# The first group of a two-layer kernel as eight plain products, with tile 0's parts for the store made later

## The reference, cut to what matters

```python
# x: (B, S, D); B = 2, here S = 1024 tokens, D = 256, F = 1024, E = 8
g = jnp.einsum('bsd,edf->ebsf', h, Wg)
u = jnp.einsum('bsd,edf->ebsf', h, Wu)
expert_outs = jnp.einsum('ebsf,efd->ebsd', jax.nn.silu(g) * u, Wd)
expert_output = jnp.einsum('be,ebsd->bsd', gating_probs, expert_outs)
shared = jnp.einsum('bsf,fd->bsd', jax.nn.silu(h @ Sg) * (h @ Su), Sd)
sg = shared_gate_prob[:, :, None]
return (1.0 - sg) * expert_output + sg * shared      # added to x, then layer 2
...
attn_in = jnp.tanh(jnp.einsum('bsd,da->bsa', hidden, W1) + b1)
scores = jnp.einsum('bsa,a->bs', attn_in, v)
p = jax.nn.softmax(masked_scores, axis=-1)
pooled = jnp.einsum('bjl,bld->bjd', p, hidden) / cnt[..., None]   # added again
```

## Time and profile before

| | |
|---|---|
| time, median of 3 runs | 1097.8 us (1097.63 to 1097.84) |
| the profiled execution | 1097.32 us, of which the span from first to last instruction 1095.6 us |
| busy share of the span | PE 99%, DVE 86%, ACT 68%, POOL 57% |
| matmuls | 4846 |
| DMA | 242.30 MB, 219 GB/s of HBM traffic over the span |

### The profile page before, as it was taken

How to read it: one execution, slowest core, us unless ns; L and a number is a source line. 1 busy time by engine, 2 the same in 40 slices (tenths; PEclk the granted TensorE clock), 3 DMA queues, 4 the chain that set the end, 5 groups by cost and what they waited for, 6 DMA issues and landing times.

```text
span 1095.6 us, 16016 instructions
## 1 busy us (share of the span) xinstructions
PE 1088.1 (99%) x4846; PEld 893.2 (82%) x4846; DVE 946.8 (86%) x1224; ACT 747.6 (68%) x1335; POOL 621.7 (57%) x543
## 2 busy tenths in 40 slices
PE   8999999999999999999999999999999999999998
PEld 6888888888888888888888888888878888888886
DVE  7888888888888888888689999999888999889986
ACT  7777677677777667677666666666656666666666
POOL 7765666656766665656335566555543444454435
PEclk9999999999999999999999999999999999999999
DMA  7776676666676676676675566666545655555522
GB/s 240 236 275 222 241 268 244 241 259 226 240 269 234 252 261 222 243 269 250 259 250 211 212 214 207 207 216 219 201 164 198 212 205 186 209 210 198 196 104 78
DMA packets 82421, 242.30 MB, mean 221 GB/s; under 512 B 23456, under 2 KB 54688, under 8 KB 73120
## 3 DMA queue, kind: packets, MB, share of 16 engines
q1 hardware_dynamic: 81520, 240.75, 61.4%
q10 hardware_dynamic: 816, 0.52, 0.2%
HBM read 134.29 MB, written 105.91 MB: 219 GB/s over the span
## 4 chain that ended last, share of the span: by engine, by line
PE 97%; POOL 1%; DVE 1%; DMA 0%; issue 0%; ACT 0%; ACTq 0%; DVEq 0%; POOLq 0%
PE acc_of L1769 11%; PE acc_of L1771 11%; PE acc_of L1770 11%; PE v_both L1769 9%; PE v_both L1771 9%; PE v_both L1770 9%; PE g_ps L1769 6%; PE e_ps L1769 6%; PE g_ps L1771 6%; PE e_ps L1771 6%; PE g_ps L1770 6%; PE e_ps L1770 6%; DMA raw<-in_L_cond_Wg 0%; POOL raw L645 0%; PE acc_of L2005 0%
## 5 line engine op out<-in xcount | busy, mean ns | idle before, releaser
L1023 ACT ACTIVATE silu<-g_ps 128x512 f32<-128x512 f32 x144 | 86.2, 599 | 171.2 <-PE g_ps L1771 171.0
L1769 PE MATMUL v_both<-xs_hi,wq 128*128 128x512 f32 x432 | 168.6, 390 | 0.1
L1771 PE MATMUL v_both<-xs_lo,wq 128*128 128x512 f32 x432 | 168.1, 389 | 0.0
L1770 PE MATMUL v_both<-xs_hi,wq 128*128 128x512 f32 x432 | 168.1, 389 | 0.0
L1386 DVE TENSOR_TENSOR up<-v_both,p_sb 128x512 f32<-128x512 f32 x144 | 99.2, 689 | 46.2 <-PE v_both L1771 43.1
L848 POOL TENSOR_TENSOR a<-a,a_own 128x512 f32<-128x512 f32 x35 | 56.1, 1604 | 132.4 <-DVE a_own L1413 132.4
L1341 DVE TENSOR_TENSOR wq<-raw,wq 128x896 fp32r<-128x896 f32 (+1 forms) x70 | 123.7, 1768 | 0.0
L1379 DVE TENSOR_TENSOR gate<-e_ps,v_part 128x512 f32<-128x512 f32 x144 | 98.6, 684 | 28.9 <-PE e_ps L1771 27.9
L1029 ACT ACTIVATE p_sb<-e_ps 128x512 f32<-128x512 f32 x144 | 86.3, 599 | 53.4 <-PE e_ps L1771 53.1
L1769 PE MATMUL e_ps<-xs_hi,wq 128*128 128x512 f32 x288 | 112.4, 390 | 0.7 <-POOL wq L640 0.7
L1769 PE MATMUL g_ps<-xs_hi,wq 128*128 128x512 f32 x288 | 112.5, 391 | 0.4 <-ACT v_both L1017 0.4
(11 more groups left out here) (298 smaller groups left out, 2861.2 us busy)
## 6 DMA issues: line engine op xcount, KB each, us to landing
wq_kept<-wq SPq DMA_DIRECT2D x72, 896.0 KB, 4.6
wq<-wq_kept SPq DMA_DIRECT2D x72, 896.0 KB, 4.5
wd_kept<-wd SPq DMA_DIRECT2D x36, 1024.0 KB, 6.5
wd<-wd_kept SPq DMA_DIRECT2D x36, 1024.0 KB, 6.2
raw_d<-in_L_cond_Wd SPq DMA_DIRECT2D x32, 256.0 KB, 4.5
raw<-in_L_cond_Wg SPq DMA_DIRECT2D x31, 256.0 KB, 2.6
raw<-in_L_cond_Wu SPq DMA_DIRECT2D x31, 256.0 KB, 3.3
out_x<-x SPq DMA_DIRECT2D x8, 256.0 KB, 2.1
```

The lines of the kernel that those rows point to most:

```text
L1023: nc.scalar.activation(silu0[:, i % 2, :], g_ps[:], ACT.Silu).then_inc(silu0_done, 1)
L1769: nc.tensor.matmul(ps, w_hi, a_hi, start=start, stop=False, skip_group_check=True)
L1770: nc.tensor.matmul(ps, w_lo, a_hi, start=False, stop=False, skip_group_check=True)
L1771: return nc.tensor.matmul(ps, w_hi, a_lo, start=False, stop=stop, skip_group_check=True)
```

## The change

Group 0 is computed by eight plain products (`first_group`): gate and up of tile 0 for both halves of tokens, with the blocks of Wg, Wu and x as they are. Gate goes to `g_ps` and `e_ps`, up to `v_ps[0]` and to the bank `acc[1][1]`. It needs no sums of x and none of weights. The split blocks of Wu lie in slot 2 of `wq` (`UP0`), a split x block in `h_hi`/`h_lo` (`X21`). p1 of group 1 stands between the third and the fourth pair of products. Then p2, p7 and p6 of group 1 follow, and the loop starts at i = 1. Since group 0 has no p7 and p6 to keep, the counts of several semaphores shift by one.

On GpSimd the split of Wu comes in the place of tile 0's sums, and the sums of both tiles of pair 0 are made by one `combine`. The five other parts of tile 0 are needed in batch 1 only. They are made after the low parts of tile 2, in a place of their own (`w0_parts`, where x lay before its transposition), and SyncE stores them from there. SyncE stores the first two parts at n = 0, waits at n = 1 for the five others, stores them, and then loads pair 2. ScalarE's and VectorE's lists at the start are written in another order, and VectorE's `rest_w` and ScalarE's `round_w` of tile 1 come before the loop.

```diff
+        w0_parts = place("w0_parts", [P, 2, NP - 2, P], F32R, l1_at[1])
...
+        UP0 = [w[:, 0:2, :] for w in weights(2)]
+        UP0_BANK = acc[1][1]
+        X21 = h_hi[1][:, 2, :], h_lo[1][:, 2, :]
...
-        ROUNDED = ((1, 2, 4, 7, 6, 5, 3), (1, 2, 7, 6, 4, 5, 3))
-        COPIED = (1, 4, 2)
+        ROUNDED = ((1, 2, 0, 4, 5, 7, 6, 3), (1, 2, 7, 6, 4, 5, 3))
+        COPIED = (1, 2, 4)
...
-                sp.wait_ge(gu_split, n + 1)
+                if n == 0:
+                    sp.wait_ge(gu0_split, 1)
+                    sp.dma_start(wq_kept[0][:, :, 0:2, :], wq[:, 0, :, 0:2, :].bitcast(F32)).then_inc(wq_stored[0], 16)
+                    continue
+                sp.wait_ge(gu_split, n)
+                if n == 1:
+                    sp.wait_ge(gu0_split, 3)
+                    sp.dma_start(wq_kept[0][:, :, 2:NP, :], w0_parts[:].bitcast(F32)).then_inc(w0_stored, 16)
                 if n % PAIR == PAIR - 1 and m < NU // PAIR:
                     load_gu(sp, m)
...
+                if n == 0:
+                    sp.wait_ge(w0_stored, 16)
...
-                combine(s, slice(0, P))
-                split(w[:, 3:8, :], hi[:, 2:NP, :], lo[:, 2:NP, :], NP - 2, gu_hi_done, 1, gu_split)
+                split(w[:, 0:4:3, :], UP0[0], UP0[1], 2, gu0_hi_done, 2, gu0_split)
                 pool.wait_ge(staged_g[s], 16)
                 pool.wait_ge(staged_u[s], 16)
-                combine(s, slice(P, PAIR * P))
+                combine(s, slice(0, PAIR * P))
...
-                    pool.wait_ge(gu_hi_done, PAIR + 1)
-
-                    pool.wait_ge(gu_split, PAIR)
+                    pool.wait_ge(gu_hi_done, PAIR)
+                    pool.wait_ge(gu_split, PAIR - 1)
                     nc.gpsimd.tensor_tensor(lo[:], raw[:, 1, 1:8, 0:P], hi[:].bitcast(F32), ALU.subtract).then_inc(gu_split, 1)
+                    pool.wait_ge(xT_done, KD * NT)
+                    split(raw[:, 0, 3:8, 0:P], w0_parts[:, 0], w0_parts[:, 1], NP - 2, gu0_hi_done, 3, gu0_split)
...
-                act.wait_ge(t_step, 3 * (n // PAIR + 2 if n >= PAIR else n + 1))
+                act.wait_ge(t_step, 3 * (n // PAIR + 1))
+                if n == 2:
+                    act.wait_ge(p_done[3], 1)
...
+            def gate_second(i):
+                if i == 0:
+                    act.wait_ge(p_done[4], 1)
+                else:
                     act.wait_ge(gate1_done, i)
-                nc.scalar.activation(v_part[:], v_ps[i % 2][:], ACT.Copy).then_inc(v_copied, 1)
-
-            def gate_second(i):
-                act.wait_ge(gate1_done, i + 1)
-                if i:
                     act.wait_ge(h_done[1], i)
-                nc.scalar.activation(silu1[:], gate1[:], ACT.Silu).then_inc(silu1_done, 1)
+                nc.scalar.activation(silu1[:], gate1[:] if i else e_ps[:], ACT.Silu).then_inc(silu1_done, 1)
...
+            act.wait_ge(xT_done, KD + 1)
+            nc.scalar.activation(X21[0], acc[0][1][:], ACT.Copy).then_inc(xs_hi_done[0], 1)
             act.wait_ge(xs_split[0], 1)
             copy_xT(0, BLOCK[1])
-            copy_xT(0, BLOCK[4])
+            round_x(0, 4)
+            act.wait_ge(staged_g[0], 16)
+            nc.scalar.activation(weights(1)[0][:, 0:2, :], raw[:, 0, 1:3, P:PAIR * P], ACT.Copy).then_inc(gu1_hi_done, 1)
             act.wait_ge(xs_split[0], 2)
             copy_xT(0, BLOCK[2])
-            seed(0)
-            round_x(0, 4)
+            gate_first(0)
+            round_x(0, 5)
+            act.wait_ge(xs_split[0], ROUNDED[0].index(4) + 1)
+            copy_xT(0, BLOCK[4])
             round_x(0, 7)
-            act.wait_ge(staged_g[0], 16)
-            nc.scalar.activation(weights(1)[0][:, 0:2, :], raw[:, 0, 1:3, P:PAIR * P], ACT.Copy).then_inc(gu1_hi_done, 1)
-            gate_first(0)
+            round_w(1)
             round_x(0, 6)
-
-            act.wait_ge(s_done[0], SQ[6] + 1)
-            round_x(0, 5)
-            keep_p7(0)
-            round_x(0, 3)
-            keep_v(0)
-            round_w(1)
 
             ROUND_X1 = {X1_AT + 8 + 2 * k: (q,) for k, q in enumerate(ROUNDED[1])}
             for i in range(NU):
                 seed(i + 1)
-                if i == 1:
+                if i == 0:
+                    round_w(2)
+                elif i == 1:
                     round_w(3)
                 gate_second(i)
                 if i == 0:
-                    round_w(2)
+                    round_x(0, 3)
                 elif i == PAIR:
                     round_w(4)
                 gate_first(i + 1)
...
+            dve.wait_ge(xs_hi_done[0], ROUNDED[0].index(0) + 1)
             nc.vector.tensor_copy(half_of(0, 1, 0), acc[0][1][:]).then_inc(xT_own, 1)
-            dve.wait_ge(xT_copied, COPIED.index(4) + 1)
+            nc.vector.tensor_tensor(X21[1], acc[0][1][:], X21[0].bitcast(F32), ALU.subtract).then_inc(xs_split[0], 1)
+            dve.wait_ge(xs_hi_done[0], ROUNDED[0].index(4) + 1)
+            dve.wait_ge(xT_own, 1)
             combine_x(0, 5)
-            dve.wait_ge(xT_own, 1)
+            rest_x(0, 4)
+            dve.wait_ge(gu1_hi_done, 1)
+            nc.vector.tensor_tensor(weights(1)[1][:, 0:2, :], raw[:, 0, 1:3, P:PAIR * P],
+                                    weights(1)[0][:, 0:2, :].bitcast(F32), ALU.subtract).then_inc(gu1_split, 1)
+            dve.wait_ge(xT_copied, COPIED.index(1) + 1)
+            dve.wait_ge(xs_split[0], ROUNDED[0].index(0) + 1)
             combine_x(0, 7)
+            rest_x(0, 5)
             combine_x(0, 6)
             rest_x(0, 7)
-
+            rest_w(1)
             dve.wait_ge(xs_hi_done[0], ROUNDED[0].index(6) + 1)
             dve.wait_ge(xT_copied, COPIED.index(2) + 1)
             combine_x(0, 3)
-            for q in (6, 4):
-                rest_x(0, q)
-            dve.wait_ge(gu1_hi_done, 1)
-            nc.vector.tensor_tensor(weights(1)[1][:, 0:2, :], raw[:, 0, 1:3, P:PAIR * P],
-                                    weights(1)[0][:, 0:2, :].bitcast(F32), ALU.subtract).then_inc(gu1_split, 1)
-            rest_x(0, 5)
+            rest_x(0, 6)
...
-                second_gate(i)
                 if i == 0:
                     rest_x(0, 3)
-                second_up(i)
-                if i == 0:
-                    rest_w(1)
-                elif i <= PAIR:
+                else:
+                    second_gate(i)
+                    second_up(i)
+                if 1 <= i <= PAIR:
...
+            def first_group(first_half):
+
+                whole = xs_hi[0][:, XQ[1], :], xs_hi[0][:, XQ[2], :], X21[0], xs_hi[0][:, XQ[4], :]
+                rest = xs_lo[0][:, XQ[1], :], xs_lo[0][:, XQ[2], :], X21[1], xs_lo[0][:, XQ[4], :]
+                gate_w = [[w[:, k, :] for w in weights(0)] for k in range(KD)]
+                up_w = [[w[:, k, :] for w in UP0] for k in range(KD)]
+                if first_half:
+                    steps = ((g_ps, gate_w, 0, (1, 2)), (v_ps[0], up_w, 0, (7, 6)), (e_ps, gate_w, 1, (5, 4)))
+                else:
+                    steps = ((UP0_BANK, up_w, 1, (None, 3)),)
+                for ps, w, t, signals in steps:
+                    for k in range(KD):
+                        if ps is g_ps:
+                            pe.wait_ge(gu0_split, 1)
+                            pe.wait_ge(xs_split[0], k + 1)
+                        elif ps is v_ps[0]:
+                            pe.wait_ge(gu0_split, 2)
+                        elif ps is e_ps and k == 0:
+                            pe.wait_ge(xs_split[0], ROUNDED[0].index(0) + 1)
+                        elif ps is e_ps:
+                            pe.wait_ge(xs_split[0], ROUNDED[0].index(4) + 1)
+                        else:
+                            pe.wait_ge(xT_copied, COPIED.index(4) + 1)
+                        n = t * KD + k
+                        mm = three_pass(ps[:], *w[k], whole[n], rest[n], k == 0, k == KD - 1)
+                        if signals[k]:
+                            mm.then_inc(p_done[signals[k]], 1)
...
+                pe.wait_ge(silu0_done, i)
...
+                if i == 1:
+                    pe.wait_ge(gu_split, i)
+                    pe.wait_ge(silu1_done, 1)
+                else:
+                    pe.wait_ge(gate1_done, i - 1)
...
-            gate_start(0)
-            keep_busy(2, e_ps)
-            gate_end(0)
-            keep_busy(4, e_ps)
-            p7(0)
-            p6(0)
-            for i in range(NG):
+            first_group(True)
+            gate_start(1)
+            first_group(False)
+            gate_end(1)
+            p7(1)
+            p6(1)
+            for i in range(1, NG):
```

70 lines of the change are left out of this document (34 added, 36 removed).

## The result

The changed kernel takes 1099.71 us (median of 20 runs, 1099.04 to 1100.35), the kernel before in the same comparison 1097.64 us (20 runs, 1097.39 to 1098.54). The ratio is 1.0018, with a 95% interval from 1.0011 to 1.0024: **slower by 2.1 us**. The forecast was 1097.8 us, no change; the time lies inside the range, in the part of the rival "slower" (1098.7 to 1100.3). The profiled execution took 1099.78 us, its span is 1098.1 us (before 1095.6), the granted clock 0.999 as before. Of all the executions timed for this text one fell out, 2483.43 us in `e1_load_first`; its ratio leaves it out.

The account below looks back on a forecast made before the run. TensorE bounds the kernel, busy 97% of the span, so only its waits count. Lead -1.7 us plus new wait +1.7 gives 0.0 change: 1095.6 us span, 1097.3 execution, 1097.8 us median; range 1096.1 to 1099.9 us.

Parts of the forecast that it names:

- rival "slower": Wu lands 5 us or more after issue, or VectorE holds the sums: 1098.7 to 1100.3 us; chance 0.22.
- Part 1: TensorE's first groups: ten products without a dummy from 7.89 us, so p7(1) could start at 14.7 us if none waits.
- Part 2: p7(1) waits for ScalarE's silu behind `round_w(2)` and starts at 16.2 us instead of 17.62.
- The lead: TensorE's time won in the first groups: 1.7 us at most, at p2(2) (20.2 instead of 21.92), capping the gain.
- Part 3: Tile 0's five remaining parts on GpSimd, 1.33 and 1.52 us, end at 20.7 us.
- Part 4: SyncE's queue: Wu issued at 21.7 behind the wait and store, lands at 26.1; pair 2's sums end at 29.4 us.
- it decides at 29.4: End of pair 2's sums, in us, at which the marker stays at 36.15; later ends make the kernel slower.
- Part 5: From the end of pair 2's sums through ScalarE and VectorE to the marker: 6.75 us, giving 36.15 us.
- the marker: Product p2 of group 4 into `g_ps`, at 36.15 us before; the whole was to shift as it does.
- Behind the marker the chain has slack again: After group 4's p2 nothing comes late: the next pair's sums are needed only at about 40 us, five after they come.
- PE waiting beyond 45 us for Wd parts or pair 3's sums: Sign that the prediction is wrong: slower by a mechanism it had priced at nothing.
- The clock rival: The granted clock falls at the new wait at p7(1), the start's longest; given little chance, no row prices it.

Follow-up runs that it names:

- e1_load_first: Changed kernel with pair 2's loads issued ahead of the store of tile 0's five parts, still behind the wait for them; 1099.21 us.
- e3: Changed kernel without GpSimd's making of tile 0's five parts and SyncE's wait for them, other bytes stored instead (batch 1's tile 0 not right); 1097.95 us.
- e4: Changed kernel with GpSimd making tile 0's five parts ahead of tile 2's low parts instead of behind them; 1098.38 us.
- e5: Changed kernel with one of the five parts stored early, GpSimd making four, and pair 2's loads and tile 1's store ahead of the wait; 1097.13 us.
- e2: Changed kernel with pair 2's loads issued also behind tile 1's store of 896 KB; 1101.82 us.
- e10: e5 with SyncE's order put back: wait, store of the parts (512 instead of 640 KB), then pair 2's loads; 1097.78 us.
- e9: Kernel before the change, with pair 2's loads issued late, behind the store of tile 2; 1098.42 us.

## Why the prediction was wrong, point by point

**Part 1 held.** Ten products back to back; from the first product they needed the 6.8 us that were counted. The first one started 0.86 us later than assumed, in this execution; in the others it lies between 7.64 and 8.73.

**Part 2 held, but for 0.5 us.** p7(1) was expected at 16.2 us and came at 16.70; the order on ScalarE is as described. `round_w(2)` did not start when the sums were done (14.66) but at 15.16, `[0.45 <-PE acc_of L1791]`: it waits for p3 of the first group as well, which the prediction had passed over, though the listing of ScalarE's order names it (`[waits p3_done,t_step]`). In this execution PE had begun late; where it began earlier, at 8.13 us in e3 and 7.64 in e4, the sums were done at 15.2 and 15.0 us, and p7(1) started at 16.69 and 16.52 all the same. **The lead was mis-sized**: 1.7 us were taken at p2(2), 1.27 were there (20.65 against 21.92), and at p2(3) only 0.80, because the chain of VectorE and ScalarE behind `v_part` holds PE at 25.67 us. I had taken the lead at p2(2) to last.

**Part 3 ended at 21.12 instead of 20.7**, by the same late `round_w(2)` (0.45 us). Its own 2.85 us were right.

**Part 4 is the step that failed.** That the load, not GpSimd, starts the sums was right; the end of pair 2's sums was mis-sized, 29.4 us where 30.98 were measured, and each of its terms was too small. These are the rows of SyncE and of GpSimd:

```profile
21.25 0.55 SPq L577 DMA_DIRECT2D wq_kept<-w_parts  x1
21.84 0.61 SPq L507 DMA_DIRECT2D raw<-in_L_cond_Wg  x1
22.50 1.01 SPq L507 DMA_DIRECT2D raw<-in_L_cond_Wu  x1
```

```profile
27.32 1.29 POOL L658 TENSOR_TENSOR raw<-raw 128x512 f32<-128x512 f32 x1 [2.20 <-DMA raw<-in_L_cond_Wu]
...
30.98 0.74 POOL L692 TENSOR_TENSOR raw_d<-raw_d 128x256 f32<-128x256 f32 x1
```

Wu was issued at 22.50, not 21.7: 0.42 comes from part 3, and SyncE began 0.13 us behind the parts and took 1.25 us, not 0.9, for the store and Wg. (The prediction's own terms, 20.7 + 0.5 + 0.4, give 21.6; it wrote 21.7, which hid 0.1 us of this.) The landing took 4.7 us, not 4.4, the sums 3.66, not 3.3, and from landing to start 0.13 was not counted. Together 0.8 + 0.3 + 0.1 + 0.4 = 1.6 us: 30.98 instead of 29.4. The landing and the sums lay within their bounds (3.0 to 5.5 and 3.08 to 4.19), but all terms erred on the same side, and the forecast stood on the very edge at which the case turns ("it decides at 29.4"). It gave 0.22 to what happened and 0.48 to the edge.

**Part 5 held.** From the sums' end to the marker 6.43 us, where 6.75 was taken; the edge was at 29.7 instead of 29.4.

**What was priced at nothing.** "Behind the marker the chain has slack again" failed. The prediction had named something near it as a sign of being wrong, PE waiting beyond 45 us for Wd parts or pair 3's sums; the wait came at 43.40 us, for `v_part`. VectorE in group 4, first two rows of the kernel before, then three of the changed kernel:

```profile
36.01 0.95 DVE L1413 SCALAR_TENSOR_TENSOR h<-silu,gates,up 128x512 f32<-128x512 f32 x1 [0.33 <-ACT silu L1041]
...
38.98 0.74 DVE L1434 SCALAR_TENSOR_TENSOR v_both<-silu,gates,v_both 128x512 f32<-128x512 f32 x1
```

```profile
37.93 1.53 DVE L1434 SCALAR_TENSOR_TENSOR h<-silu,gates,up 128x512 f32<-128x512 f32 x1 [1.20 <-ACT silu L1059]
39.39 2.18 DVE L1355 TENSOR_TENSOR wq<-raw,wq 128x896 fp32r<-128x896 f32 x1
41.49 0.74 DVE L1455 SCALAR_TENSOR_TENSOR v_both<-silu,gates,v_both 128x512 f32<-128x512 f32 x1
```

ScalarE's seed was at 36.76 instead of 34.83, so it was 1.9 us late where PE was 1.26 late: its 0.7 us of slack was spent. VectorE's `h` then started at 37.93 instead of 36.01 and took 1.53 us instead of 0.95. It ran beside GpSimd's low parts of Wd:

```profile
37.63 1.29 POOL L678 TENSOR_TENSOR wd<-raw_d,wd 128x512 fp32r<-128x512 f32 x1
```

This instruction follows pair 3's sums, which GpSimd had started late too, at 34.56 after a wait for the same kind of load (`[1.05 <-DMA raw<-in_L_cond_Wu]`; before they stood from 30.40 to 34.4, and the low parts of Wd at 35.11, 0.9 us ahead of `h`). In both kernels, as in e5, `h` ends 0.54 or 0.55 us behind GpSimd's instruction. The 896-wide low parts came 2.5 us late, and PE waited 0.70 us more. I had looked at when pair 3's sums are *needed*, not at what follows them on GpSimd and whom that would run beside. In the sum: -0.80 of lead at p2(3), +2.06 of waiting in group 3, +0.70 in group 4, 1.96 us. Against the forecast of no change: +1.58 at the sums' end (Part 4), -0.32 from there to the marker (Part 5), +0.70 behind it; the lead does not enter, since the sums came later than PE.

The rival "slower" had the mechanism, its point and its size (+0.9 at 30.3 to +2.5 at 31.9; 30.98 gives +1.6 by its 6.75 us, and 1.26 were measured, since the way to the marker took 6.43). The clock rival was rightly put low for this kernel.

## What to carry to other kernels

When work is moved behind another engine's queue, walk the DMA queue that waits for it: a load that stands behind the new wait and a store moves with them, and here a load that had landed nearly three microseconds ahead of its use became the one that everything waits for. When a forecast puts a moved chain exactly at the edge where it begins to cost, add up the small terms (a second semaphore at a wait, issue time of each DMA, start after landing) before calling it even, since each is positive. Earlier is not always better: sums made early (e3) fell on VectorE's instructions, and the fastest version has freed loads with GpSimd's order as it was.

## What the runs showed of the hardware

**Behind one long wait the granted clock fell.** In the profiled execution of e2 PE waited 3.32 us for `p_sb`. Below are this row and the stretches behind it (engines' busy us with the number of instructions, then the granted clock, DMA share, GB/s):

```profile
35.34 0.79 PE L1791 MATMUL e_ps<-xs_hi,wq 128*128 128x512 f32 x1 [3.32 <-ACT p_sb L1047]
```

```profile
32.00:34.00 2.00, 0.02 (x1) 0.00 (x0) 0.17 (x1) 1.15 (x2) 1.76 (x4) 1.00 1.12 430
34.00:36.00 2.00, 0.66 (x2) 0.56 (x3) 2.00 (x3) 1.49 (x4) 1.84 (x3) 0.69 0.63 263
36.00:38.00 2.00, 2.00 (x6) 1.59 (x5) 2.00 (x3) 2.00 (x4) 1.84 (x2) 0.50 1.01 333
38.00:40.00 2.00, 2.00 (x6) 1.54 (x5) 0.94 (x2) 1.79 (x4) 1.80 (x2) 0.50 1.14 235
40.00:42.00 2.00, 2.00 (x7) 1.52 (x7) 1.91 (x3) 0.00 (x0) 2.00 (x3) 0.61 0.10 15
42.00:44.00 2.00, 2.00 (x10) 1.68 (x9) 2.00 (x2) 1.12 (x2) 1.84 (x3) 1.00 0.00 0
```

The granted clock went to 0.50, the lower of its two levels (1.2 of 2.4 GHz), and PE did 6 matmuls in 2 us instead of 9 or 10. The marker came at 41.76 us, where sums' end + 6.43 gives 39.33: 2.4 us on top of the wait. That execution took 1103.45 us and the median is 1101.82, so I don't claim that every execution of e2 had it. That the wait made the clock fall is read from the order of events in this one execution. PE's wait of 1.32 us in the changed kernel left the mean at 0.999.

**A load behind stores on one queue is slow, and so is issuing it.** Pair 2's Wu of 256 KB landed 2.9 us after its issue with only Wg just ahead of it (e1), 4.0 behind a store of 512 KB (e10), 4.7 behind 640 KB (the changed kernel), 5.5 behind 896 KB (e9) and 6.3 behind 640 and 896 KB (e2); pair 3's in the changed kernel, behind two more stores, after 6.8. Each is from one execution. SyncE's time for one load rose from about 0.4 us to 1.4 (rows of the changed kernel's DMA issues, then of SyncE):

```profile
raw<-in_L_cond_Wg SPq DMA_DIRECT2D x1, 256.0 KB, 7.5
raw<-in_L_cond_Wu SPq DMA_DIRECT2D x1, 256.0 KB, 6.8
```

```profile
27.56 1.40 SPq L507 DMA_DIRECT2D raw<-in_L_cond_Wu  x1
```

The Trainium skill, DMA: Bandwidth & Descriptors, section "Queues, rings and completion order", has the descriptors of a queue start in the ring's order. The trace agrees: in the changed kernel the store issued at 21.25 us landed after 3.8 us, Wg of 21.84 after 4.6 and Wu of 22.50 after 4.7, in the order of their issue. It adds the price here: 1.1 us for 512 KB ahead, 1.8 for 640 KB, 2.6 for 896 KB.
